# Joining a router's marks into codes with 16-bit operations of ScalarE and VectorE in place of matmuls, and decoding them in the expert stage

## What is computed

```
logits[t, o, 0..7] = h[t] @ router_w[o*8 + e] + router_b[o*8 + e]
w, sel = top_k(softmax(logits), 2);  w = w / sum(w)
c[t, e] = sum over o of (w of e at o, where e is one of the two chosen)
out[t, o] = x[t, o] + sum over e of c[t, e] * (h[t] @ expert_w[e, o] + expert_b[e, o])
```

## Time and profile before

| | |
|---|---|
| median of 3 runs | 2481.45 us (2475.61 to 2482.29) |
| the profiled execution's own time | 2476.82 us |
| its span in the profile | 2475.0 us |
| mean granted clock of TensorE | 0.985 |
| TensorE matmul busy | 2380.4 us (96%) |
| VectorE busy | 1611.1 us (65%) |
| ScalarE busy | 1107.4 us (45%) |
| mean DMA traffic | 66 GB/s |

### The profile page before, as it was taken

One profiled execution on the slowest core, in us unless ns is written; L12 is line 12 of the kernel. 1 busy time (PEld: TensorE's weight loads), 2 busy tenths in 40 slices (PEclk: granted clock), 3 DMA queues, 4 the chain that ended last, 5 costly groups with the idle time before them and its releaser, 6 DMA issues.

```text
span 2475.0 us, 31344 instructions
## 1 busy us (share of the span) xinstructions
PE 2380.4 (96%) x10800; PEld 1948.4 (79%) x10800; DVE 1611.1 (65%) x2469; ACT 1107.4 (45%) x1486; POOL 8.9 (0%) x16
## 2 busy tenths in 40 slices
PE   5889999999999996999999999999799999999999
PEld 3568888888888885888888888888588888888887
DVE  7973434343343435688888888889886667666763
ACT  5652323233332324677777767777532222222221
POOL 0000000000000000000000000000000000000000
PEclk9899999999999998999999999999899999999999
DMA  4221111120211016010111101101622211222220
GB/s 144 80 98 52 53 34 53 34 69 18 69 53 51 34 34 237 26 69 34 51 43 41 51 34 51 51 34 51 225 77 76 76 65 63 75 76 76 76 68 21
DMA packets 102164, 162.49 MB, mean 66 GB/s; under 512 B 11634, under 2 KB 44914, under 8 KB 101874
## 3 DMA queue, kind: packets, MB, share of 16 engines
q1 hardware_dynamic: 51490, 105.44, 12.5%
q10 hardware_dynamic: 50640, 56.63, 6.9%
HBM read 111.71 MB, written 50.33 MB: 65 GB/s over the span
## 4 chain that ended last, share of the span: by engine, by line
PE 87%; DVE 7%; ACT 2%; DMA 1%; issue 1%; SPq 1%; ACTq 0%; POOL 0%; DVEq 0%; POOLq 0%
PE slot L1132 18%; PE ex L1288 9%; PE ex L1290 9%; PE ex L1292 9%; PE pj L1142 9%; PE plane L1252 8%; PE plane L1256 8%; PE plane L1254 8%; PE slot L1182 3%; PE code L1236 2%; PE slot L1108 1%; PE slot L1171 1%; DVE lead_in L1005 1%; DMA rraw<-in_rwT 1%; PE slot L1161 0%
## 5 line engine op out<-in xcount | busy, mean ns | idle before, releaser
L1288 PE MATMUL ex<-ew_hi,hb 128*128 128x512 f32 x1024 | 401.6, 392 | 19.0 <-DVE ew_lo L1028 12.4
L1252 PE MATMUL plane<-rw_hi,hb 128*128 128x512 f32 x1024 | 406.4, 397 | 12.3 <-ACT plane L631 12.3
L1132 PE MATMUL slot<-y_hi,wgu 128*128 128x512 f32 x1024 | 404.0, 395 | 8.7 <-ACT wpj L514 8.3
L1132 PE MATMUL slot<-y_lo,wgu 128*128 128x512 f32 x1024 | 400.9, 391 | 0.0
L1290 PE MATMUL ex<-ew_hi,hb 128*128 128x512 f32 x1024 | 400.7, 391 | 0.0
L1292 PE MATMUL ex<-ew_lo,hb 128*128 128x512 f32 x1024 | 400.4, 391 | 0.0
L1256 PE MATMUL plane<-rw_lo,hb 128*128 128x512 f32 x1024 | 399.9, 390 | 0.0
L1254 PE MATMUL plane<-rw_hi,hb 128*128 128x512 f32 x1024 | 399.3, 390 | 0.0
L716 ACT ACTIVATE ex<-eb_sb 128x512 f32<-128x512 f32 x248 | 149.3, 602 | 458.2 <-DVE acc L1067 392.2
L1005 DVE SCALAR_TENSOR_TENSOR lead_in<-code_in,wts 128x1024 bf16<-128x1024 bf16 x256 | 311.6, 1217 | 3.2 <-ACT wts L665 1.5
L797 DVE TENSOR_TENSOR hid<-gate,slot 128x512 f32<-128x512 f32 x128 | 88.0, 688 | 260.7 <-ACT gate L523 260.5
(11 more groups left out here) (116 smaller groups left out, 3173.4 us busy)
## 6 DMA issues: line engine op xcount, KB each, us to landing
hb<-h_scratch SPq DMA_DIRECT2D x34, 512.0 KB, 3.6
h_scratch<-ht ACTq DMA_DIRECT2D x64, 256.0 KB, 3.1
hb<-h_scratch ACTq DMA_DIRECT2D x30, 512.0 KB, 3.7
q_raw<-in_w_ffn SPq DMA_DIRECT2D x24, 512.0 KB, 3.4
x_mix<-in_x SPq DMA_DIRECT2D x8, 1024.0 KB, 5.4
x_scratch<-x_res ACTq DMA_DIRECT2D x8, 1024.0 KB, 4.4
rraw<-in_rwT SPq DMA_DIRECT2D x8, 1024.0 KB, 10.3
lead_scratch<-lead SPq DMA_DIRECT2D x32, 256.0 KB, 2.1
```

The lines of the kernel that those rows point to most:

```text
L1132: last = mm(slot[s % 2][:, g, :], wgu[:, c, r * P:(r + 1) * P], y[:, c, :], start=(c == 0 and v == 0), stop=(c == DC - 1 and v == 1))
L1252: mm(plane[b][:, :, :], hb[:, u, c, 0, :], rw_hi[:, w, c, o], start=False, stop=False, skip_group_check=True)
L1288: mm(ex[e][:, :], hb[:, u, c, 0, :], ew_hi[:, e, c, :], start=(first and c == 0), stop=False, skip_group_check=True)
```

## The change

- The one Relu of `stand` becomes four of 512 elements, one for each pair of experts (q = 0 to 3), with scale 255 x STEP[q] and bias STEP[q] (128, 32, 8, 2), written as unsigned 16-bit integers. A mark of pair q is then 256 x STEP[q], STEP[q] or 0.
- VectorE's `join` ORs the marks of experts 0 to 3 with those of experts 4 to 7 (128 x 1024, 16 bits) into `half_code`. It stands in the next half, behind the tenth of its 12 steps. `highest`, `others` and `keep` leave the router stage; so do `codes` on TensorE, `pow_id`, and the two PSUM banks.
- `half_code` goes to DRAM once for each half, 4 x 256 numbers of 16 bits for a row. SyncE's queue has three writes for a tile: half 0, lead, half 1, each behind a wait of its own. Each tile's codes take 512 KB both ways, before 256 KB.
- In the expert stage VectorE's `decode(n + 2)` stands between `expert(n, 0)` and `total(n + 2, 0)`: five operations in a chain. `half_in` has one buffer; SyncE loads it again when `decoded` says that it was read.
- The 16 totals of tiles 0 and 1, and the two decodes, are dealt out one behind each half from tile 23 on (17 halves), with the last behind them; `weigh(0)` and `weigh(1)` of ScalarE move from tile 27 to tile 23.
- Between the stages, SyncE's `spill(NT - 2, 0)` moves from behind the third pair of expert weights to behind the first; `decode_last` becomes `join(NT - 1, 1)`; the wait of expert 6 goes, and `eb_sb` waits for `joined` at 64.

```diff
+STEP = [128.0, 32.0, 8.0, 2.0]
...
+            def spill(n, u, first, both, second):
+                sp.wait_ge(joined, first)
+                spill_half(n, 0)
+                sp.wait_ge(lead_ready, both)
+                spill_lead(n, u)
+                sp.wait_ge(joined, second)
+                spill_half(n, 1)
...
-                    sp.wait_ge(code_read, chosen[u])
-                    spill(m * 2 + u, u)
+                    spill(m * 2 + u, u, *marks[u])
+            with sp.Fori(1, NT // 2 - 3) as m:
+                tiles(m)
+            sp.wait_ge(decoded, 1)
+            load_halves(1)
...
-                if b == 2:
-                    sp.wait_ge(code_read, 2 * (NT - 1))
-                    spill(NT - 2, 0)
+                if b == 0:
+                    spill(NT - 2, 0, 2 * NT - 3, 2 * NT - 2, 2 * NT - 2)
             load_h(1, 1)
-            sp.wait_ge(code_read, 2 * NT)
+            sp.wait_ge(joined, 2 * NT)
             sp.dma_start(xin[:, 0, :], X1T[0]).then_inc(x1_in[0], 16)
             sp.dma_start(eb_sb[:, :, :], eb).then_inc(eb_in, 16)
...
+            def ahead_choices(n, u, wait, ready):
+                sp.wait_ge(decoded, ready)
+                load_halves(n + 3)
                 sp.wait_ge(summed, wait)
-                load_choices(n + 3, 1 - u)
+                load_lead(n + 3, 1 - u)
...
                 nc.scalar.activation(sgn[:, s, :], flat, ACT.Sign).then_inc(signs, 1)
-                act.wait_ge(signs, n * 4 + (2 * s + 1))
-                nc.scalar.activation(sgn[:, s, :], sgn[:, s, :], ACT.Relu, scale=255.0, bias=one_col[:, :]).then_inc(signs, 1)
+                act.wait_ge(signs, n * 2 + (s + 1))
+                for q in range(4):
+                    at = slice(2 * q * HO, (2 * q + 2) * HO)
+                    nc.scalar.activation(sgn[:, s, at].bitcast(U16), sgn[:, s, at], ACT.Relu,
+                                         scale=255.0 * STEP[q], bias=step_col[:, q:q + 1]).then_inc(placed, 1)
...
-            for e in range(E):
-                nc.vector.tensor_scalar(pow_id[:, e, :], ident[:, :], float(2 ** (E - e)), None, ALU.mult).then_inc(b_const, 1)
+            for q in range(4):
+                nc.vector.memset(step_col[:, q:q + 1], STEP[q]).then_inc(b_const, 1)
...
+            def join(n, s):
+                dve.wait_ge(placed, n * 8 + 4 * (s + 1))
+                if not (isinstance(n, int) and n == 0):
+                    dve.wait_ge(half_out[s], n * 16)
+                bits = sgn[:, s, :].bitcast(U16).rearrange("p (e n) -> p e n", e=E)
+                tt(half_code[:, s, :, :], bits[:, 0:4, :], bits[:, 4:8, :], ALU.bitwise_or).then_inc(joined, 1)
+            def decode(n, k):
+                u = k % 2
+                dve.wait_ge(half_in_done, n * 16 + 16)
+                tt(half_in[:, :, 0:2, :], half_in[:, :, 0:2, :], half_in[:, :, 2:4, :], ALU.bitwise_or).then_inc(dec, 1)
+                dve.wait_ge(dec, n * 4 + 1)
+                nc.vector.scalar_tensor_tensor(digits[:, 1, :].rearrange("p (s n) -> p s n", s=2), half_in[:, :, 0, :], 2.0,
+                                               half_in[:, :, 1, :], ALU.mult, ALU.add).then_inc(dec, 1)
+                dve.wait_ge(dec, n * 4 + 2)
+                nc.vector.tensor_scalar(digits[:, 0, :].bitcast(I32), digits[:, 1, :].bitcast(I32), FIELD, None,
                                         ALU.bitwise_and).then_inc(dec, 1)
...
+                dve.wait_ge(dec, n * 4 + 3)
+                tt(digits[:, 1, :], digits[:, 1, :], digits[:, 0, :], ALU.subtract).then_inc(dec, 1)
+                dve.wait_ge(dec, n * 4 + 4)
+                if not (isinstance(n, int) and n < 2):
+                    dve.wait_ge(summed, n * E - E)
                 upper = digits[:, :, :].bitcast(U16).rearrange("p a (n b) -> p a n b", b=2)[:, :, :, 1]
...
+                nc.vector.tensor_scalar(code_in[:, u, :, :].bitcast(U16), upper, FOLD, None,
+                                        ALU.bitwise_and).then_inc(decoded, 1)
...
                 after(9)
                 step(tt(m2[:, :], m2[:, :], low4[:, 0, :], ALU.max))
-                if decode:
-                    dve.wait_ge(dec, before(1))
-                    others(chosen)
+                if joins:
+                    join(n if s else n - 1, 1 - s)
...
-            sums = [(n, e) for n in range(2) for e in range(E)]
-            for n in range(NT - 5, NT):
+            early = [(n, e) for n in range(2) for e in [None] + list(range(E))]
+            for n in range(NT - 9, NT):
...
+                        if e == 0:
+                            decode(n + 2, (k + 2) % 4)
                         total(n + 2, e, (k + 2) % 4)
...
-            def codes(n, s):
-                pe.wait_ge(signs, n * 4 + (2 * s + 2))
-                if not (isinstance(n, int) and n == 0):
-                    pe.wait_ge(code_read, n * 2 + (s - 1))
-                for e in range(E):
-                    last = mm(code[s][:, 0, :], pow_id[:, e, :], sgn[:, s, e * HO:(e + 1) * HO],
-                              start=(e == 0), stop=(e == E - 1))
-                last.then_inc(code_done, 1)
```

More of the change, by code:

```diff
@@ L213, in build @@
         sgn = sb("sgn", [P, 2, E * HO], BF16, p2)
-        slot_code = sb("slot_code", [P, 2, 2, D], U16, p2)
-        digits = sb("digits", [P, 2, HO], F32, p2)
+        half_code = sb("half_code", [P, 2, 4, HO], U16, p2)
         plane = [pb(f"plane{s}", [P, 2, HO], p2) for s in range(4)]
-        spare = [pb(f"spare{s}", [P, 2, HO], p2) for s in range(2)]
-        code = [pb(f"code{s}", [P, 2, HO], p2) for s in range(2)]
         p2.close()
@@ L399, in _, with tiles @@
                 load_h(2 + u, u)
-                sp.wait_ge(code_read, (u + 1) * 2)
-                spill(u, u)
-            sp.wait_ge(spilled, 64)
-            load_choices(0, 0)
-            load_choices(1, 1)
-            with sp.Fori(1, NT // 2 - 1) as m:
+                spill(u, u, 2 * u + 1, 2 * u + 2, 2 * u + 2)
+            for u in range(2):
+                sp.wait_ge(lead_out[u], 16)
+                load_lead(u, u)
+            for s in range(2):
+                sp.wait_ge(half_out[s], 32)
+            load_halves(0)
+            def tiles(m):
                 left = [sp.snap(m * (2 * PT) + (u + 1) * PT) for u in range(2)]
-                chosen = [sp.snap(m * 4 + (u + 1) * 2) for u in range(2)]
+                marks = [[sp.snap(m * 4 + (2 * u + k)) for k in (1, 2, 2)] for u in range(2)]
                 for u in range(2):
@@ L676, in _ @@
             router(2, 0)
-            with act.Fori(1, NT // 2 - 3) as m:
+            with act.Fori(1, NT // 2 - 5) as m:
                 router(m * 2 + 1, 1)
@@ L681, in _ @@
             weigh(1, 1, 0)
-            for n in range(NT - 5, NT - 1):
+            for n in range(NT - 9, NT - 1):
                 router(n, n % 2)
@@ L929, in half @@
+            def half(n, s, u, trip, joins=True):
                 cnt = [0]
@@ L937, in after @@
                     dve.wait_ge(tour, n * (2 * KT) + (s * KT + k))
-                ps = 1 - s
-                pu = u if s == 1 else 1 - u
-                do = slice(ps * HO, (ps + 1) * HO)
-                chosen = code[ps][:, 0, :]
-                def before(k):
-                    return n * (2 * KD) + ((s - 1) * KD + k)
                 dve.wait_ge(evac, n * PT + 4 * (s + 1))
@@ L975, in half, with router @@
                 if s == 0 and not (isinstance(n, int) and n < 2):
-                    dve.wait_ge(spilled, n * 32 - 32)
+                    dve.wait_ge(lead_out[u], trip * 16)
                 tt(lead[:, u, s * HO:(s + 1) * HO], m1[:, :], m2[:, :], ALU.subtract).then_inc(lead_ready, 1)
-                if decode:
-                    if s == 1 and not (isinstance(n, int) and n < 2):
-                        dve.wait_ge(spilled, n * 32 - 32)
-                    dve.wait_ge(dec, before(KD))
-                    dve.wait_ge(lead_ready, n * 2 + (s + 1))
-                    keep(pu, ps)
-            def decode_last():
-                k = (2 * NT - 1) * KD
-                dve.wait_ge(code_done, 2 * NT)
-                highest(code[1][:, 0, :])
-                dve.wait_ge(dec, k + 1)
-                others(code[1][:, 0, :])
-                dve.wait_ge(dec, k + 2)
-                keep(1, 1)
-            def router(n, u):
-                half(n, 0, u)
-                half(n, 1, u)
+            def router(n, u, trip):
+                half(n, 0, u, trip)
+                half(n, 1, u, trip)
             def total(n, e, k):
@@ L1007, in total @@
                     ALU.is_equal, ALU.mult, accum_out=c_ring[:, k, e:e + 1]).then_inc(summed, 1)
-            half(0, 0, 0, decode=False)
-            half(0, 1, 0)
-            router(1, 1)
-            router(2, 0)
-            with dve.Fori(1, NT // 2 - 3) as m:
-                router(m * 2 + 1, 1)
-                router(m * 2 + 2, 0)
-            sums = [(n, e) for n in range(2) for e in range(E)]
-            for n in range(NT - 5, NT):
```

(30 more changed lines are left out.)

75 lines of the change are left out of this document (35 added, 40 removed).

## The result

The changed kernel takes 2415.6 us (median, 2411.72 to 2416.33), the kernel before 2479.5 in the same comparison: a ratio of 0.974, 95% interval 0.9722 to 0.9759. I had forecast 2412 us in a range of 2404 to 2422. The profiled execution took 2416.33 us with a span of 2414.5; I had 2409.3 for the span. The gain between the two medians is 63.9 us, where I had 65.7.

The account below looks back on a forecast made before the run. TensorE, busy 96% of the span, was taken as the bound. Codes 58.9 plus passage 6.8 make 65.7 us, taking the profiled 2476.82 to 2411.1; forecast 2412 us, range 2405 to 2417, or 2404 to 2422 with two rivals.

Parts of the forecast that it names:

- The codes: 58.9 us: Router stage, TensorE: removing the code matmuls saves 0.95 us in each of 62 halves, 58.9 us.
- ScalarE: 9.1 of 10.88 us: Router stage: four small Relus add 0.7 us a half, so ScalarE's 9.1 us of work fits in 10.88.
- C: Router stage, `stand`: the four small Relus make ScalarE pace every half; 36 us slower, 2515 us; chance 0.03.
- D: Router stage: the 58.9 us go over into waits for ScalarE, quarters near 1.33 us; no change, 2478 us; chance 0.02.
- VectorE: 9.2 of 10.88, join not waited for: Router stage: with a join of 0.69 us VectorE's half takes 9.2 us of 10.88, its marks ready 0.9 us early.
- Rival A: VectorE's 16-bit ORs run at one element a cycle; 8.4 us given back from tile 23 and passage, 2420 us; chance 0.12.
- From tile 23: Late router stage: one sum or decode behind each half leaves VectorE at most 1.8 us late; cost nothing.
- my signs of being wrong: Router stage: halves over 11 us, a join of 1.2 us, or `stand` released by VectorE from tile 23.
- SyncE's queue: Spills and loads land in time; at the passage weights stand behind the last join: nothing, at most 2 us.
- Passage: 6.8 us: Router to experts: earlier `eb_sb` gains 8.0 us, decode before the second bank loses 1.2; net 6.8 us.
- Rival B: Router to experts: passage gives nothing, weights behind the moved spill or `eb_sb` slower; 2419 us; chance 0.07.
- Expert stage: nothing: Expert stage: decodes raise VectorE to 18 to 19.4 of a tile's 21.8 us; delayed bank wanted 19 us later; no cost.

Follow-up runs that it names:

- one-matmul kernel: The kernel before with one of the eight code matmuls of a half left, waits and decoding kept: 2436.5 us, ratio 0.9831.
- marks twice: The changed kernel with the four small Relus of each half done twice, first into a scratch tile: 2483.0 us, ratio 1.0013 to the kernel before.
- join-twice kernel: The changed kernel with every join done twice, the first into a scratch tile: 2424.5 us.
- two items a half: The changed kernel with its 18 early decodes and sums dealt two behind each half from tile 27, not one from tile 23: 2424.8 us.
- second profile: The changed kernel run again with no edit: 2414.1 us, of which 721.8 from the last plane to the end.
- biases behind: The changed kernel with spill back, tile 2's decode and sums behind tile 0's expert steps, and bias products behind seven of those steps: 2411.2 us.

## Why the prediction was right, and where it was off

**The number.** The sum was 65.7 us, and the medians differ by 63.9. The forecast of 2412 us took this sum from a profiled execution that was 4.6 us faster than the median, and then added 0.9 of these 4.6 without a reason; 2481.45 - 65.7 = 2415.8 would have met 2415.6, but by luck: beside the changed kernel the median of before was 2479.5, and from there the sum is 1.8 us too large.

**The codes: 58.9 us.** Right: the router stretch went from 744.5 to 685.4, 59.1 us. The distances 11.83 and 10.88 of the earlier trace rows held for all 62 halves but for the places named above. That the price was TensorE's own time is shown by the one-matmul kernel.

**ScalarE: 9.1 of 10.88 us.** Right: 214.92 / 260 x 10.88 = 9.0. The quarters took 0.71 us each, 2.46 for the four. That its room is what was taken for granted is shown by the marks twice: at 11.9 us a half it becomes the pace. Rivals C and D had this right, place and price: the doubled marks are a q of 5.34 / 4 = 1.33 us, for which C's 6.5 + 4q gives 11.8 us a half (measured 11.87) and D no gain (2478 forecast, 2483.0 measured). D's 2478 doesn't follow from its own terms, though: it takes back the passage's gain too.

**VectorE: 9.2 of 10.88, join not waited for.** Right within 0.2. Rival A fell with the 0.684 us of the join. A delay of 0.6 us in each half costs nothing until tile 23, and 9 to 10 us from there on. Rival A had most of it in the passage; in the join-twice kernel it came half and half, 5.7 us in the router stretch and 5.6 behind it.

**From tile 23.** The dealing-out costs nothing, as forecast (no gap of TensorE in the router stage), and it is worth some 9 us against two items a half. That is more than a side effect: without it a seventh of the gain is lost. But one of my signs of being wrong did appear: `stand` is released by VectorE, in three halves. The half with the decode took 12.6 us (12.7 forecast), so it left VectorE 1.7 late, not too late for the 2.5 us that I had free. What I missed is that the two `weigh`, 3.4 us of ScalarE just before, hold up the evacuation that VectorE's half starts from by 1.64 us (12.52 - 10.88). Both together are 3.3 us, and `stand` waited 0.99. ScalarE's own 3.9 us took that up, so TensorE saw nothing of it.

**SyncE's queue: "Nothing, at most 2 us".** This is the term that was mis-sized; it measures 2.5 us. I looked at when the second pair of weights is issued (-4.3 forecast, -3.0 measured) and left out that the spill's three writes, 768 KB, go ahead of it: by an estimate at the 374 GB/s of the earlier trace rows these are 2.1 us. (The -5.5 that I gave for the kernel before was wrong as well: its second pair left at -6.4.) The third split came 2.46 us late, and the edit that puts the spill back takes that away.

**Passage: 6.8 us.** 4.2 measured in the profile, 5.9 in the second one. Up to the start of tile 1's second bank both had gained 6.0 to 6.1 us (52.3 us after the last plane before, 46.3 and 46.2 now); in the first profile the clock then took back 1.7, which is inside the 3 us that I had given it. `eb_sb` left 2.8 us later than forecast, by the third split; from there to the restart it was 15.6 us, not 16.9, as the load was faster. The decode in front of expert(0, 1) took 3.4 us (3.5), and TensorE waited 2.14 or 0.77 us (1.2): VectorE has the second bank ready 5.14 us after the first in both, and how much of that is a wait depends on how fast TensorE does the first bank. Rival B, that the passage gives nothing, is refuted: as its own counter-argument had it, the wait for the code matmul is gone.

**Expert stage: nothing.** Right: VectorE is busy 400.48 of 510 us, 17.1 of a tile's 21.8 (18 to 19.4 forecast), and TensorE for all 510.

**Start of the program.** Forecast 0. In the profiled execution the first evacuation came at 997.53, not 994.73, and so 2.8 us of the 5.2 by which the span missed are there. In the second profile it came at 994.91. It is scatter and not the change's.

## What to carry to other kernels

Where one engine is the pace and two of its stages differ only in one piece of work, the distance of the same event in a stage with it and one without it is the price of that piece; sum it over the stages, and then ask of each other engine whether its work fits in the shorter period, not in the old one. Work dealt out over more halves can be what keeps the new period; count it in the item's length against the slack of a half. Where a queue's steps are reordered at a passage between stages, count the bytes that go ahead as well as the moment of issue, and look at what the first engine to be fed waits for. And where two profiles differ by a few us, compare the times of one event after the other: here that told the 2.5 us of an edit from the 1.7 us that the clock added at another place.

## What was not expected of the hardware

After a wait of TensorE of 3.99 us, twice with the same instructions, the first matmul took 0.77 us (a 1.2 GHz start) in one execution and 0.47 in the other; in the latter the matmuls behind it still went to 0.63 us, the lower level, for some us. The rest of the two executions differs by 1.7 us, so the passage can't be forecast closer than that from waits alone. Where the 1.7 us lie is seen in the traces. Up to the second bank of tile 1 both take the same (46.3 and 46.2 us from the last plane); from there to the end it is 677.2 us in the first and 675.6 in the second. In the first, nine matmuls ran 0.43 us apart, and not 0.23, right behind the wait of 2.14 us for that bank. In the second, the slow spell came in the bank before it, where TensorE would only have waited the longer: there it cost nothing. Six of the seven edited versions of the changed kernel have 675.5 to 675.8 us from that bank on; "biases behind", with its wait at tile 2, has 679.1. A scratch Relu chained to the one before it on the same engine took 0.72 us from start to start (2.89 for four), against 0.61 for four that need not wait.
